# Local attention in a gated cross-attention network: where the inverse norms of the query and key heads are computed, and when their unit vectors are made

## The chip, the cores and the metric

The kernel runs on one core of one Trainium2 chip. A core has TensorE (PE in the profile), VectorE (DVE), ScalarE (ACT), GpSimd (POOL) and SyncE (SP, which here issues the DMAs). The metric is the device time of one execution, in microseconds (us). The kernel before took 3235.11 us, the median of three runs from 3233.68 to 3237.66.

## The reference, cut to what matters

Two gated cross-attentions and a feed-forward network come first. The last part, in which the change lies, is a local transformer of two layers on 2048 tokens of 256 features, with 8 heads of 64 and windows of 128 tokens. Its attention does this:

```python
qkv = shift_token(x) @ wqkv                      # 256 -> 3 * 512
q, k, v = heads(qkv)
q = q / clip(norm(q), 1e-12) * q_scale           # k likewise
q, k = rotary_xpos(q, k)                         # x*cos*scale + rotate_half(x)*sin*scale
# window w attends to its own 128 keys and those of window w-1
sim = mask(8 * q_w @ [k_{w-1}, k_w].T)
o_w = softmax(sim) @ [v_{w-1}, v_w]
x = x + concat(o) @ wo
```

After it comes a gated feed-forward network, and then the second layer.

## The kernel before, in words

The local transformer is `local_transformer`, and its attention is `windowed_attention`, called once per layer. Tokens lie on the 128 partitions, one window per tile (`Z[:, w, :]`), and a window is the unit of work: 16 of them in each layer. Each engine has a program of its own, written out in Python in the order in which it is to run. The engines meet only through semaphores (`s["..."]`); `after(engine, name, count)` is a wait, and `.then_inc` a signal. The order of the calls in each engine's loop `for w in range(ST + 1)` (ST is 16) therefore sets the order of the work. Iteration w works on several windows at once: it projects window w+3, rotates w+2, turns w+1, scores w, and adds the result of w-1.

The path of one window through the engines:

- PE turns the tokens (`turn_input`, L1983), ACT copies them out of PSUM (`move_input`, L2093 and L2097), and POOL splits them into a high and a low fp16 part (`split_input`, L67 and L71).
- PE projects queries and keys (`project_qk`, L77 to L79) into two PSUM banks; ACT squares the 1024 numbers of a token (`square`, L2104); DVE sums the squares of each of the 16 heads into `norms[:, 0, :]` (`sum_squares`, L2238).
- ACT takes the root of these 16 numbers (`root`, L2124). Square root and exponential need different activation tables, so a table load stands before the root and another before the next exponential.
- DVE clips, inverts and multiplies (`make_unit`, L2177, L2179, L2182); the unit vectors are 128x1024. With this the PSUM banks are free for the next projection.
- DVE multiplies them by the cosine table (`straighten`, L2223), POOL by the sine table (`cross`, L2310), and DVE adds the two (`rotate`, L2245). PE turns the result (`turn`, L1974) and ACT copies it as `qT` and `kT` (`move`, L2085 and L2086).
- PE scores (`score`, L1934, or L1939 where the two key tiles are not neighbours in the ring); DVE masks and takes the maxima, in two groups of four heads (`mask` L2206, `maxima` L2214); ACT takes the exponentials with their sums (`expo`, L2071).
- DVE inverts the eight sums (`invert`, L2191) and POOL spreads them over 64 columns a head (`expand`, L2331). PE turns this by four matmuls against the identity (`spread`, L2026), and ACT copies it (`move_spread`, L2079).
- PE turns the probabilities (`turn_probs`, L2002), ACT copies them (`move_probs`, L2117), and PE applies them to the values (`apply`, L2016).
- DVE multiplies the output by the spread inverses (`normalize`, L2198), PE mixes it with `wo` (`mix`, L1990), and DVE adds it to the tokens (`add`, L2231).

In iterations 2 to 10 DVE also splits one part of the feed-forward weights into high and low fp16 (`split_weights`: L59 and L63).

Of the kernel before, what the change touches and what calls it, by code (L numbers as in the profile page):

```python
# [1440 lines left out]
def narrow_attention(nc, m, rows_d, ctxT_d, wq_d, wk_d, wv_d, wo_d, bqk_d, bv_d, bo_d, q_parts, k_parts, pw):  # L1441
# [390 lines left out]


V_RING, K_RING, Z_RING = 6, 4, 3

RAW, W1_PARTS, W2_PARTS = 3, 6, 3
SPLIT_AT = range(2, 2 + W1_PARTS + W2_PARTS)
# [2 lines left out]
HEAD_AT = [4 * (p // 4) + 2 * (p % 2) + (p // 2) % 2 for p in range(LH)]  # L1840
ATTENTION_SIGNALS = (
    "scored", "qk_projected", "v_projected", "turned", "spread", "in_turned", "mixed", "probs_turned", "applied",
    "exped", "spread_moved", "moved", "in_moved", "squared", "valued", "probs_moved", "rooted",
    "clipped", "inverted", "united", "weighed", "expanded", "normed", "masked", "maxed", "straightened", "added", "summed",
    "rotated", "crossed", "in_split", "in_hi", "tables_in", "rest_in", "scaled", "cleared")


# [37 lines left out]
def windowed_attention(nc, m, name, Z, pw, wm, w, l, s):  # L1885

    base = l * ST
    with ExitStack() as own:
# [8 lines left out]
        unit = [sb(f"unit{i}", [P, 2, LH, 2, LD // 2]) for i in range(2)]  # L1897
        straight, crossed = sb("straight", [P, 2, LH, LD]), sb("crossed", [P, 2, LH, 2, LD // 2])
        rotated = [sb(f"rotated{i}", [P, 2 * INNER]) for i in range(2)]
        norms = sb("norms", [P, 4, 16])  # L1900
        scores, probs = sb("scores", [P, LH, 2 * P]), sb("probs", [P, LH, 2 * P])
        probsT = [sb(f"probsT{i}", [P, 4, 2, P]) for i in range(2)]
        minus_max, sums, inverse = sb("minus_max", [P, LH]), sb("sums", [P, LH]), sb("inverse", [P, LH])
# [7 lines left out]
        def after(engine, sem, count):  # L1911
            if count > 0:
                engine.wait_ge(s[sem], count)

        with nc.Block() as block:
# [5 lines left out]
            def _(pe):  # L1921
# [55 lines left out]

                def turn_input(w):

                    after(pe, "normed", base + w - 4)  # L1980
                    after(pe, "in_moved", base + w)
                    for k in range(DK):
                        last = nc.tensor.transpose(m.PS[:, OUT_BANK, k * P:(k + 1) * P], Z[:, w, k * P:(k + 1) * P], m.ident[:])  # L1983
                    last.then_inc(s["in_turned"], 1)
# [57 lines left out]
                for w in range(ST + 1):  # L2042
                    if inside(w):
                        score(w)
                    if inside(w + 3):
                        project_qk(w + 3)
                    if inside(w - 1):
                        if w == 1:
                            pe.wait_ge(s["rest_in"], 32 * (l + 1))
                        mix(w - 1)  # L2050
                    if inside(w + 1):
                        turn(w + 1)
                    if inside(w + 3):
                        project_v(w + 3)
                    if inside(w + 4):
                        turn_input(w + 4)
                    if inside(w):
                        for g in range(2):
                            turn_probs(w, g)
                        apply(w)  # L2060
                        spread(w)

            @block.scalar
            def _(act):
# [10 lines left out]
                def move_spread(w):  # L2075

                    after(act, "spread", base + w + 1)
                    after(act, "normed", base + w)
                    nc.scalar.activation(spread_in[:].rearrange("p c n -> p (c n)"), m.PS[:, OUT_BANK, :],  # L2079
                                         ACT.Copy).then_inc(s["spread_moved"], 1)  # L2080
# [49 lines left out]
                value(0)  # L2130
                root(0)
                move_input(2)
                square(1)
                value(1)
                root(1)
                move_input(3)
                square(2)
                move(0)
                value(2)
                root(2)  # L2140
                for w in range(ST + 1):
                    if inside(w - 1):
                        move_spread(w - 1)
                    if inside(w):
                        expo(w, 0)
                        expo(w, 1)
                    if inside(w + 1):
                        move(w + 1)
                    if inside(w + 4):
                        move_input(w + 4)  # L2150
                    if inside(w + 3):
                        square(w + 3)
# [6 lines left out]
                    if inside(w + 3):  # L2159
                        root(w + 3)  # L2160

            @block.vector
            def _(dve):
# [8 lines left out]

                def make_unit(w):

                    after(dve, "rooted", base + w + 1)
                    after(dve, "united", base + w)
                    nc.vector.tensor_scalar(norms[:, 2, :], norms[:, 1, :], 1e-12 * FF_SCALE, None, ALU.max).then_inc(s["clipped"], 1)  # L2177
                    dve.wait_ge(s["clipped"], base + w + 1)
                    nc.vector.reciprocal(norms[:, 3, :], norms[:, 2, :]).then_inc(s["inverted"], 1)  # L2179
                    dve.wait_ge(s["inverted"], base + w + 1)  # L2180
                    after(dve, "crossed", base + w - 1)
                    nc.vector.tensor_tensor(  # L2182
                        unit[w % 2][:].rearrange("p q h a d -> p (q h) (a d)"),
                        m.PS[:, qk_bank(w):qk_bank(w) + 2, :].rearrange("p b (h d) -> p (b h) d", d=LD),
                        norms[:, 3, :].unsqueeze(2).to_broadcast([P, 16, LD]), ALU.mult).then_inc(s["united"], 1)

                def invert(w):

# [45 lines left out]
                def sum_squares(w):  # L2234

                    after(dve, "squared", base + w + 1)
                    after(dve, "clipped", base + w)
# [27 lines left out]
                dve.wait_ge(s["tables_in"], 32 * (l + 1))  # L2265
                scale_tables(0, 2)
                scale_tables(2, ST)
                sum_squares(0)
                for w in (0, 1):
                    make_unit(w)  # L2270
                    straighten(w)
                    sum_squares(w + 1)
                    rotate(w)
                for w in range(ST + 1):
                    if inside(w + 2):
                        make_unit(w + 2)
                    if inside(w - 1):
                        normalize(w - 1)
                    if inside(w):
                        if w == 0:  # L2280
                            dve.wait_ge(s["rest_in"], 32 * (l + 1))
                        for g in range(2):
                            mask(w, g)
                            maxima(w, g)
                    if inside(w - 1):
                        add(w - 1)
                    if inside(w + 2):
                        straighten(w + 2)
                    if inside(w + 2):
                        rotate(w + 2)  # L2290
                    if inside(w):
                        invert(w)
                    if inside(w + 3):
                        sum_squares(w + 3)
                    if w in SPLIT_AT:
                        split_weights(SPLIT_AT.index(w))

            @block.gpsimd
            def _(pool):
                nc.gpsimd.memset(kT[:, :, K_RING - 1, :], 0.0)  # L2300
                nc.gpsimd.memset(V[:, V_RING - 1, :, :], 0.0).then_inc(s["cleared"], 1)

                def cross(w):
# [21 lines left out]
                def expand(w):  # L2325
# [11 lines left out]
                split_input(1)  # L2337
                split_input(2)
                cross(0)
                cross(1)  # L2340
                split_input(3)
                for w in range(ST + 1):
                    if inside(w + 2):
                        cross(w + 2)
                    if inside(w):
                        expand(w)
                    if inside(w + 4):
                        split_input(w + 4)


LN_PARTS = ("shifted", "shift_moved", "first_half", "counted", "step", "root_wanted", "root_done", "staged", "h_turned",
# [425 lines left out]
```

## Time and profile before

| | |
|---|---|
| median of three runs | 3235.11 us |
| the profiled execution's own time | 3229.91 us |
| its span | 3227.8 us |
| PE busy over the span | 2967.1 us (92%) |
| DVE busy | 2208.0 us (68%) |
| ACT busy | 1982.0 us (61%) |
| POOL busy | 218.4 us (7%) |

The span is the stretch from the first to the last recorded instruction of the profiled execution, and its own time lies 2.1 us above it. The busy shares are means over stages with different limits. The attention of the two local layers stands from about 2424 to 2702 us and again from about 2822 to 3099 us, minus the feed-forward part between. In a timeline each row gives the start, the duration, the engine, the line, the operation, what it writes and reads, the number of instructions merged in it, and in brackets how long the engine had idled before and what released it.

### The profile page before, as it was taken

Reading aid. Unit: us, or ns where it says so; the run is one execution under the profiler, and the core shown is the slowest. Engines: PE = TensorE matmul, PEld = TensorE weight load, DVE = VectorE, ACT = ScalarE, POOL = GpSimd, SP = SyncE. Lnnn points to the kernel's source line nnn. Section 1 sums busy time; section 2 is a strip of 40 time slices with the busy share of each in tenths; the row PEclk is TensorE's granted clock in tenths of the full one; section 3 lists DMA queues with packets and bytes.
Section 4 is the critical chain, followed back from the end, with each engine's and each line's share of the span. In section 5 each row is a group of like instructions: output and inputs, shape, how many; then the busy total and the mean of one; then the engine's idle time right before and its main releaser. Section 6 shows DMA issues by size and latency. Waiting matters only on the chain. (4 is left out here: it accounts for less than half of the span.)

```text
span 3227.8 us, 71016 instructions
## 1 busy us (share of the span) xinstructions
PE 2967.1 (92%) x29442; PEld 1483.9 (46%) x29442; DVE 2208.0 (68%) x2752; ACT 1982.0 (61%) x2682; POOL 218.4 (7%) x325
## 2 busy tenths in 40 slices
PE   6999999999999999999999887999977887988878
PEld 3444444444444444444444563222235665556655
DVE  6888788878888888878788854000027775677756
ACT  5665655655656656556556424999965773267732
POOL 0000000000000000000000102000004223042200
PEclk8999999999999999999999898999998998999989
DMA  2000000000000000000000003110010001000000
GB/s 78 7 2 2 8 2 8 2 2 8 2 2 8 2 2 8 2 3 2 2 3 2 31 3 126 27 36 27 28 44 20 17 1 58 3 16 17 1 1 27
DMA packets 30033, 51.65 MB, mean 16 GB/s; under 512 B 6071, under 2 KB 22538, under 8 KB 28554
## 3 DMA queue, kind: packets, MB, share of 16 engines
q1 hardware_dynamic: 29706, 46.91, 4.6%
q8 instruction: 252, 4.13, 0.5%
q14 instruction: 75, 0.61, 0.1%
HBM read 41.04 MB, written 5.83 MB: 15 GB/s over the span
## 5 line engine op out<-in xcount | busy, mean ns | idle before, releaser
L734 ACT ACTIVATE a_probs<-PS 128x1024 f32<-128x1024 f32 x928 | 949.1, 1024 | 601.2 <-PE PS L489 597.4
L502 PE MATMUL PS<-a_probs,a_V 64*64 64x512 f32 x7424 | 977.8, 590 | 5.0 <-DVE a_heads_outT L915 3.6
L956 DVE TENSOR_TENSOR a_prob_sums<-a_prob_sums,a_probs 128x1024 f32<-128x1024 f32 x512 | 627.1, 1225 | 153.8 <-ACT a_probs L734 137.8
L953 DVE SCALAR_TENSOR_TENSOR a_prob_sums<-a_probs,a_valid,a_prob_sums 128x1024 f32<-128x1024 f32 x384 | 480.4, 1251 | 70.2 <-ACT a_probs L734 60.3
L489 PE MATMUL PS<-a_Q_hi,a_K_hi 64*64 64x512 f16 x3712 | 383.9, 381 | 5.0 <-ACT a_probs L734 4.7
L1772 ACT ACTIVATE c_probs<-PS 128x1024 f32<-128x1024 f32 (+1 forms) x416 | 382.8, 1080 | 8.3 <-PE PS L1691 6.7
L489 PE MATMUL PS<-a_Q_lo,a_K_hi 64*64 64x512 f16 x3712 | 383.5, 377 | 2.5 <-issue 2.5
L489 PE MATMUL PS<-a_Q_hi,a_K_lo 64*64 64x512 f16 x3712 | 381.1, 377 | 1.3 <-issue 1.3
L502 PEld LDWEIGHTS PS<-a_probs,a_V 64*64 64x64 f32 x7424 | 288.5, 133 | 164.1 <-issue 20.4
L489 PEld LDWEIGHTS PS<-a_Q_hi,a_K_hi 64*64 64x64 f16 x3712 | 118.4, 106 | 275.8 <-issue 270.7
L489 PEld LDWEIGHTS PS<-a_Q_hi,a_K_lo 64*64 64x64 f16 x3712 | 119.0, 107 | 228.3 <-issue 226.4
L1711 PE MATMUL PS<-c_probs,c_Vh 128*32 128x512 f32 (+1 forms) x1664 | 222.5, 607 | 0.3 <-ACT c_probs L1772 0.3
L1790 DVE COPY c_outT<-PS 128x512 f32<-128x512 f32 x16 | 11.1, 691 | 303.3 <-PE PS L1711 303.3
L1691 PE MATMUL PS<-c_Qop,c_Kop 64*128 64x512 f16 (+1 forms) x832 | 155.6, 390 | 34.6 <-ACT c_probs L1772 11.3
L2071 ACT ACTIVATE d_probs<-d_scores,d_minus_max 128x256 f32<-128x256 f32 x256 | 127.0, 497 | 88.2 <-DVE d_minus_max L2214 88.2
L489 PEld LDWEIGHTS PS<-a_Q_lo,a_K_hi 64*64 64x64 f16 x3712 | 120.0, 107 | 92.7 <-issue 7.8
L1691 PEld LDWEIGHTS PS<-c_Qop,c_Kop 64*128 64x128 f16 (+1 forms) x832 | 38.7, 94 | 250.9 <-ACT c_probs L1772 236.8
L923 DVE RECIPROCAL a_inverse<-PS 128x128 f32<-128x128 f32 x128 | 121.5, 950 | 27.1 <-PE PS L512 27.1
L71 POOL TENSOR_TENSOR b_W_lo<-b_W1T,b_W_hi 128x256 f16<-128x256 f32 x8 | 8.1, 1044 | 1830.9 <-DVE b_W_hi L67 1830.9
L2002 PE MATMUL PS<-ident,d_probs 128*128 128x128 f32 x512 | 70.3, 296 | 48.2 <-ACT d_kT L2086 41.5
L2310 POOL TENSOR_TENSOR d_crossed<-d_unit,d_tables 128x256 f32<-128x256 f32 x128 | 92.7, 758 | 147.8 <-DVE d_unit L2182 147.8
L2002 PEld LDWEIGHTS PS<-ident,d_probs 128*128 128x128 f32 x512 | 62.2, 153 | 56.2 <-issue 48.3
(325 smaller groups left out, 4227.5 us busy)
## 6 DMA issues: line engine op xcount, KB each, us to landing
c_Qop<-q_part SPq DMA_DIRECT2D x96, 64.0 KB, 2.3
c_Kop<-k_part SPq DMA_DIRECT2D x96, 50.0 KB, 2.0
d_raw<-in_l1f_w_dram SPq DMA_DIRECT2D x18, 256.0 KB, 3.2
d_tables<-in_rotary_dram SPq DMA_DIRECT2D x2, 2048.0 KB, 11.0
X<-in_x_dram SPq DMA_DIRECT2D x2, 1024.0 KB, 9.5
out_dram<-X SPq DMA_DIRECT2D x4, 512.0 KB, 3.5
c_cT<-in_ctxT_dram SPq DMA_DIRECT2D x1, 1601.0 KB, 6.4
a_probs<-in_ctx_dram SPq DMA_DIRECT2D x3, 512.0 KB, 5.0
```

What stands on the lines that cost most here:

```text
L489: last = nc.tensor.matmul(m.PS[64 * g:64 * g + 64, 2 * (n % 2) + h, :], k[rows, half_keys], q[rows, queries], start=(j == 0), stop=(j == l ...
L502: last = nc.tensor.matmul(m.PS[64 * h:64 * h + 64, PVB + g, :], V[e][rows, s, 64 * h:64 * h + 64], probs[n % 4][rows, h * BANK:(h + 1) * B ...
L734: nc.scalar.activation(probs[n % 4][:], m.PS[:, b0:b0 + 2, :].rearrange("p b c -> p (b c)"), ACT.Exp).then_inc(exped, 1)
L923: nc.vector.reciprocal(inverse[:, part], m.PS[:, TOTAL, part]).then_inc(inverted, 1)
L953: nc.vector.scalar_tensor_tensor(out=sums, in0=new, scalar=valid[:, s:s + 1], in1=sums, op0=ALU.mult, op1=ALU.add).then_inc(summed, 1)
L956: nc.vector.tensor_tensor(sums, sums, new, ALU.add).then_inc(summed, 1)
L1691: last = nc.tensor.matmul(m.PS[0:r, STEP_BANKS[n] + b, :], Kop[e][rows, c0:c0 + r], Qop[e][rows, q0:q0 + BANK], start=True, stop=True)
L1711: last = nc.tensor.matmul(m.PS[32 * q:32 * q + 32, 4 + e, :], Vh[e][0:r, t % CT, :], probs[2 * (t % 2) + q // 2][0:r, (q % 2) * BANK:(q % ...
L1772: nc.scalar.activation(probs[2 * (t % 2) + hp][0:r, :], m.PS[0:r, STEP_BANKS[n]:STEP_BANKS[n] + 2, :].rearrange("p b c -> p (b c)"), ACT.E ...
L2002: last = nc.tensor.transpose(m.PS[:, SCORE_BANK + 2 * g + p // 2, at:at + P], probs[:, 4 * g + p, kt * P:(kt + 1) * P], m.ident[:])
L2071: last = nc.scalar.activation(probs[:, p, :], scores[:, p, :], ACT.Exp, bias=minus_max[:, p:p + 1], accum_out=sums[:, p:p + 1])
L2310: last = nc.gpsimd.tensor_tensor(crossed[:, qk, :, a, :], unit[w % 2][:, qk, :, 1 - a, :], tables[:, 1, w, qk, a * 32:a * 32 + 32].unsquee ...
```

## The change

The square root leaves ACT. POOL now clips the sums of squares and raises them to the power -0.5 (`power`, two instructions on 128x16), and DVE refines that by one Newton step, y(1.5 - 0.5 x y^2), in three instructions on 128x16 in place of the clip and the reciprocal. `make_unit(w + 3)` stands at the end of iteration w, where `make_unit(w + 2)` stood at the start of the iteration. DVE's `invert(w)` goes ahead of `rotate(w + 2)`. On ACT `square(w + 3)` goes ahead of `move_input(w + 4)`, `move_spread(w)` comes at the end of iteration w in place of the start of the next, and the table for the exponential is loaded before the loop. On PE `spread(w)` goes ahead of `apply(w)` and consists of transposes in place of matmuls. `turn_input` waits for `spread_moved` in place of `normed`.

```diff
-        norms = sb("norms", [P, 4, 16])
+        norms, minus_half = sb("norms", [P, 6, 16]), sb("minus_half", [P, 16])
...
-                    after(pe, "normed", base + w - 4)
+                    after(pe, "spread_moved", base + w - 4)
...
-                        last = nc.tensor.matmul(m.PS[:, OUT_BANK, c * P:(c + 1) * P],
-                                                expanded[:, c].rearrange("p e d -> p (e d)"), m.ident[:], start=True, stop=True)
+                        last = nc.tensor.transpose(m.PS[:, OUT_BANK, c * P:(c + 1) * P],
+                                                   expanded[:, c].rearrange("p e d -> p (e d)"), m.ident[:])
...
+                        spread(w)
                         apply(w)
-                        spread(w)
...
-                def root(w):
-
-                    after(act, "summed", base + w + 1)
-                    nc.scalar.activation(norms[:, 1, :], norms[:, 0, :], ACT.Sqrt).then_inc(s["rooted"], 1)
-
-                act.wait_ge(s["cleared"], 2 * (l + 1))
+                nc.scalar.preload_act_table(ACT.Exp)
+                act.wait_ge(s["cleared"], 3 * (l + 1))
...
-                    after(dve, "rooted", base + w + 1)
-                    after(dve, "united", base + w)
-                    nc.vector.tensor_scalar(norms[:, 2, :], norms[:, 1, :], 1e-12 * FF_SCALE, None, ALU.max).then_inc(s["clipped"], 1)
-                    dve.wait_ge(s["clipped"], base + w + 1)
-                    nc.vector.reciprocal(norms[:, 3, :], norms[:, 2, :]).then_inc(s["inverted"], 1)
-                    dve.wait_ge(s["inverted"], base + w + 1)
+                    squared, first, product, step, root = (norms[:, i, :] for i in range(5))
+                    steps = NORM_STEPS * (base + w)
+                    dve.wait_ge(s["powered"], base + w + 1)
+                    nc.vector.scalar_tensor_tensor(out=product, in0=squared, scalar=SQUARE_CLIP, in1=first, op0=ALU.max,
+                                                   op1=ALU.mult).then_inc(s["norm_step"], 1)
+                    dve.wait_ge(s["norm_step"], steps + 1)
+                    nc.vector.scalar_tensor_tensor(out=step, in0=first, scalar=-0.5, in1=product, op0=ALU.mult,
+                                                   op1=ALU.mult).then_inc(s["norm_step"], 1)
+                    dve.wait_ge(s["norm_step"], steps + 2)
+                    nc.vector.scalar_tensor_tensor(out=root, in0=step, scalar=1.5, in1=first, op0=ALU.add,
+                                                   op1=ALU.mult).then_inc(s["norm_step"], 1)
+                    dve.wait_ge(s["norm_step"], steps + 3)
...
-                sum_squares(0)
                 for w in (0, 1):
+                    sum_squares(w)
                     make_unit(w)
                     straighten(w)
-                    sum_squares(w + 1)
                     rotate(w)
+                sum_squares(2)
+                make_unit(2)
...
                     if w in SPLIT_AT:
                         split_weights(SPLIT_AT.index(w))
+                    if inside(w + 3):
+                        make_unit(w + 3)
...
+                def power(w):
+
+                    if w == 0:
+                        pool.wait_ge(s["cleared"], 3 * (l + 1))
+                    after(pool, "summed", base + w + 1)
+                    after(pool, "united", base + w)
+                    nc.gpsimd.tensor_scalar(norms[:, 5, :], norms[:, 0, :], SQUARE_CLIP, None, ALU.max).then_inc(s["limited"], 1)
+                    pool.wait_ge(s["limited"], base + w + 1)
+                    nc.gpsimd.tensor_tensor(norms[:, 1, :], norms[:, 5, :], minus_half[:], ALU.pow).then_inc(s["powered"], 1)
+
...
                     if inside(w + 4):
                         split_input(w + 4)
+                    if inside(w + 3):
+                        power(w + 3)
```

ACT, one iteration from the first copy after the exponentials to the next exponentials. Before:

```order
L2085 ACTIVATE d_qT<-PS 128x512
L2086 ACTIVATE d_kT<-PS 128x4x128
L2093 ACTIVATE d_zw<-PS 128x2x128
L2097 ACTIVATE d_zw<-PS 128x1
L2104 ACTIVATE d_squares<-PS 128x1024
L2117 ACTIVATE d_probsT<-PS 128x1024
L2111 ACTIVATE d_V<-PS 128x512
L2117 ACTIVATE d_probsT<-PS 128x1024
L2124 ACT_TABLE_LOAD
L2124 ACTIVATE d_norms<-d_norms 128x16
L2079 ACTIVATE d_spread_in<-PS 128x512
L2071 ACT_TABLE_LOAD
```

The same stretch of ACT after the change (the lines of the functions are one or so higher):

```order
L2086 ACTIVATE d_qT<-PS 128x512
L2087 ACTIVATE d_kT<-PS 128x4x128
L2105 ACTIVATE d_squares<-PS 128x1024
L2094 ACTIVATE d_zw<-PS 128x2x128
L2098 ACTIVATE d_zw<-PS 128x1
L2118 ACTIVATE d_probsT<-PS 128x1024
L2112 ACTIVATE d_V<-PS 128x512
L2118 ACTIVATE d_probsT<-PS 128x1024
L2080 ACTIVATE d_spread_in<-PS 128x512
```

Both table loads and the root are gone from the loop, and the squares stand ahead of the copy of the next tokens.

DVE, from the sums of squares of iteration 2 to the first mask of iteration 3. Before:

```order
L2238 TENSOR_REDUCE d_norms<-d_squares 128x16
L59 TENSOR_SCALAR d_w_hi<-d_raw 128x4x128
L63 SCALAR_TENSOR_TENSOR d_w_lo<-d_raw,d_w_hi 128x4x128
L2177 TENSOR_SCALAR d_norms<-d_norms 128x16
L2179 RECIPROCAL d_norms<-d_norms 128x16
L2182 TENSOR_TENSOR d_unit<-PS,d_norms 128x1024
L2198 TENSOR_TENSOR d_heads_outT<-PS,d_spread_in 128x512
L2206 TENSOR_TENSOR d_scores<-PS,d_masks 128x1024
```

The same stretch of DVE after the change:

```order
L2236 TENSOR_REDUCE d_norms<-d_squares 128x16
L59 TENSOR_SCALAR d_w_hi<-d_raw 128x4x128
L63 SCALAR_TENSOR_TENSOR d_w_lo<-d_raw,d_w_hi 128x4x128
L2170 SCALAR_TENSOR_TENSOR d_norms<-d_norms 128x16
L2173 SCALAR_TENSOR_TENSOR d_norms<-d_norms 128x16
L2176 SCALAR_TENSOR_TENSOR d_norms<-d_norms 128x16
L2180 TENSOR_TENSOR d_unit<-PS,d_norms 128x1024
L2196 TENSOR_TENSOR d_heads_outT<-PS,d_spread_in 128x512
L2204 TENSOR_TENSOR d_scores<-PS,d_masks 128x1024
```

In steady state DVE's sequence is the same but for three small instructions in place of two: the unit vectors stand between the same neighbours, and only what they wait for is another engine's.

POOL, one iteration. Before:

```order
L2310 TENSOR_TENSOR d_crossed<-d_unit,d_tables 128x8x32 x4
L2331 COPY d_expanded<-d_inverse 128x256 x2
L67 CAST d_zw_hi<-d_zw 128x256
L71 TENSOR_TENSOR d_zw_lo<-d_zw,d_zw_hi 128x256
L2310 TENSOR_TENSOR d_crossed<-d_unit,d_tables 128x8x32 x4
```

The same iteration of POOL after the change:

```order
L2310 TENSOR_TENSOR d_crossed<-d_unit,d_tables 128x8x32 x4
L2331 COPY d_expanded<-d_inverse 128x256 x2
L67 CAST d_zw_hi<-d_zw 128x256
L71 TENSOR_TENSOR d_zw_lo<-d_zw,d_zw_hi 128x256
L2342 TENSOR_SCALAR d_norms<-d_norms 128x16
L2344 TENSOR_TENSOR d_norms<-d_norms,d_minus_half 128x16
L2310 TENSOR_TENSOR d_crossed<-d_unit,d_tables 128x8x32 x4
```

The two instructions of `power` stand behind the split of the next tokens.

## Rows read from the trace of the kernel before

**Rows 1.** Stretches: us, busy time and instructions of each engine, granted clock, DMA.
```profile
2466.80:2651.60 184.80, 165.60 (x1346) 124.26 (x1342) 142.66 (x188) 145.61 (x334) 53.44 (x95) 1.00 0.03 10
```
**Rows 2.** Timeline of DVE, one iteration of the first layer's attention.
```profile
2511.28 1.22 DVE L2182 TENSOR_TENSOR d_unit<-PS,d_norms 128x1024 f32<-128x1024 f32 x1
...
2513.02 1.21 DVE L2206 TENSOR_TENSOR d_scores<-PS,d_masks 128x1024 f32<-128x1024 f32 x1
...
2520.81 0.19 DVE L2191 RECIPROCAL d_inverse<-d_sums 128x8 f32<-128x8 f32 x1
2522.22 1.22 DVE L2238 TENSOR_REDUCE d_norms<-d_squares 128x16 f32<-128x1024 f32 x1 [1.22 <-ACT d_squares L2104]
2523.36 0.42 DVE L59 TENSOR_SCALAR d_w_hi<-d_raw 128x512 f16<-128x512 f32 x1
2523.81 0.69 DVE L63 SCALAR_TENSOR_TENSOR d_w_lo<-d_raw,d_w_hi 128x512 f16<-128x512 f32 x1
2526.18 0.17 DVE L2177 TENSOR_SCALAR d_norms<-d_norms 128x16 f32<-128x16 f32 x1 [1.68 <-ACT d_norms L2124]
...
2526.68 1.22 DVE L2182 TENSOR_TENSOR d_unit<-PS,d_norms 128x1024 f32<-128x1024 f32 x1
```
**Rows 3.** Timeline of ACT, the same iteration.
```profile
2519.89 0.57 ACT L2085 ACTIVATE d_qT<-PS 128x512 f32<-128x512 f32 x1
...
2521.16 1.03 ACT L2104 ACTIVATE d_squares<-PS 128x1024 f32<-128x1024 f32 x1
...
2523.59 1.03 ACT L2117 ACTIVATE d_probsT<-PS 128x1024 f32<-128x1024 f32 x1
2524.64 1.28 ACT L2124 ACT_TABLE_LOAD   x1
2525.94 0.21 ACT L2124 ACTIVATE d_norms<-d_norms 128x16 f32<-128x16 f32 x1
```
**Rows 4.** Timeline of PE, the same iteration.
```profile
2521.09 1.94 PE L2002 MATMUL PS<-ident,d_probs 128*128 128x128 f32 x16 [0.73 <-ACT d_kT L2086]
2523.76 2.01 PE L2016 MATMUL PS<-d_probsT,d_V 128*64 128x128 f32 x32 [0.73 <-ACT d_V L2111]
2525.70 1.16 PE L2026 MATMUL PS<-ident,d_expanded 128*128 128x128 f32 x8
```
**Rows 5.** Timeline of POOL, first at the layer's start, then in the same iteration.
```profile
2448.42 1.52 POOL L71 TENSOR_TENSOR d_zw_lo<-d_zw,d_zw_hi 128x256 f16<-128x256 f32 x1
...
2521.76 0.40 POOL L67 CAST d_zw_hi<-d_zw 128x256 f16<-128x256 f32 x1
2522.24 0.67 POOL L71 TENSOR_TENSOR d_zw_lo<-d_zw,d_zw_hi 128x256 f16<-128x256 f32 x1
```
**Rows 6.** Timeline of DVE beside the first of the POOL rows above.
```profile
2449.35 0.63 DVE L2177 TENSOR_SCALAR d_norms<-d_norms 128x16 f32<-128x16 f32 x1
```
**Rows 7.** Groups of instructions on POOL by shape: count, busy us, mean ns, idle before.
```profile
L1384 POOL TENSOR_SCALAR f_qkv_raw<-f_qkv_raw 128x512 f32<-128x512 f32 x6 | 9.6, 1630 | 5.4 <-DMA f_qkv_raw<-in_l1f_wqkv_dram 5.4
...
L2652 POOL COPY d_shift<-ident 128x1 f32<-128x1 f32 x1 | 0.2, 250 | 0.0
```
**Rows 8.** Timeline of DVE and POOL at the start of layer one, then layer two.
```profile
2434.20 1.22 DVE L2238 TENSOR_REDUCE d_norms<-d_squares 128x16 f32<-128x1024 f32 x1 [3.95 <-ACT d_squares L2104]
...
2437.50 3.73 POOL L2310 TENSOR_TENSOR d_crossed<-d_unit,d_tables 128x256 f32<-128x256 f32 x4 [0.29 <-DVE d_unit L2182]
...
2451.44 1.21 DVE L2206 TENSOR_TENSOR d_scores<-PS,d_masks 128x1024 f32<-128x1024 f32 x1
...
2833.34 0.18 DVE L2177 TENSOR_SCALAR d_norms<-d_norms 128x16 f32<-128x16 f32 x1 [1.18 <-ACT d_norms L2124]
```
**Rows 9.** Timeline of PE and DVE in the last iterations of layer one.
```profile
2663.23 2.64 PE L2016 MATMUL PS<-d_probsT,d_V 128*64 128x128 f32 x32
2665.80 1.16 PE L2026 MATMUL PS<-ident,d_expanded 128*128 128x128 f32 x8
...
2668.24 1.21 DVE L2206 TENSOR_TENSOR d_scores<-PS,d_masks 128x1024 f32<-128x1024 f32 x1
```

More of the change, by code:

```diff
@@ L1834 @@
 V_RING, K_RING, Z_RING = 6, 4, 3
+NORM_STEPS, SQUARE_CLIP = 3, (1e-12 * FF_SCALE) ** 2
 RAW, W1_PARTS, W2_PARTS = 3, 6, 3
@@ L1842 @@
     "scored", "qk_projected", "v_projected", "turned", "spread", "in_turned", "mixed", "probs_turned", "applied",
-    "exped", "spread_moved", "moved", "in_moved", "squared", "valued", "probs_moved", "rooted",
-    "clipped", "inverted", "united", "weighed", "expanded", "normed", "masked", "maxed", "straightened", "added", "summed",
+    "exped", "spread_moved", "moved", "in_moved", "squared", "valued", "probs_moved",
+    "norm_step", "limited", "powered", "united", "weighed", "expanded", "normed", "masked", "maxed", "straightened", "added", "summed",
     "rotated", "crossed", "in_split", "in_hi", "tables_in", "rest_in", "scaled", "cleared")
@@ L2130, in _ @@
                 value(0)
-                root(0)
                 move_input(2)
@@ L2134, in _ @@
                 value(1)
-                root(1)
                 move_input(3)
@@ L2139, in _ @@
                 value(2)
-                root(2)
                 for w in range(ST + 1):
-                    if inside(w - 1):
-                        move_spread(w - 1)
                     if inside(w):
@@ L2148, in _ @@
                         move(w + 1)
+                    if inside(w + 3):
+                        square(w + 3)
                     if inside(w + 4):
                         move_input(w + 4)
-                    if inside(w + 3):
-                        square(w + 3)
                     if inside(w):
@@ L2158, in _ @@
                         move_probs(w, 1)
-                    if inside(w + 3):
-                        root(w + 3)
+                        move_spread(w)
             @block.vector
@@ L2184, in make_unit @@
                         m.PS[:, qk_bank(w):qk_bank(w) + 2, :].rearrange("p b (h d) -> p (b h) d", d=LD),
-                        norms[:, 3, :].unsqueeze(2).to_broadcast([P, 16, LD]), ALU.mult).then_inc(s["united"], 1)
+                        root.unsqueeze(2).to_broadcast([P, 16, LD]), ALU.mult).then_inc(s["united"], 1)
                 def invert(w):
@@ L2236, in sum_squares @@
                     after(dve, "squared", base + w + 1)
-                    after(dve, "clipped", base + w)
+                    after(dve, "united", base + w)
                     nc.vector.tensor_reduce(norms[:, 0, :], squares[:], AX.X, ALU.add).then_inc(s["summed"], 1)
@@ L2267, in _ @@
                 scale_tables(2, ST)
-                sum_squares(0)
                 for w in (0, 1):
+                    sum_squares(w)
                     make_unit(w)
                     straighten(w)
-                    sum_squares(w + 1)
                     rotate(w)
+                sum_squares(2)
+                make_unit(2)
                 for w in range(ST + 1):
-                    if inside(w + 2):
-                        make_unit(w + 2)
                     if inside(w - 1):
@@ L2288, in _ @@
                         straighten(w + 2)
+                    if inside(w):
+                        invert(w)
                     if inside(w + 2):
                         rotate(w + 2)
-                    if inside(w):
-                        invert(w)
                     if inside(w + 3):
@@ L2300, in _ @@
                 nc.gpsimd.memset(kT[:, :, K_RING - 1, :], 0.0)
+                nc.gpsimd.memset(minus_half[:], -0.5).then_inc(s["cleared"], 1)
                 nc.gpsimd.memset(V[:, V_RING - 1, :, :], 0.0).then_inc(s["cleared"], 1)
@@ L2334, in expand @@
                     last.then_inc(s["expanded"], 1)
+                def power(w):
[6 more added lines that the diff above has]
+                    nc.gpsimd.tensor_tensor(norms[:, 1, :], norms[:, 5, :], minus_half[:], ALU.pow).then_inc(s["powered"], 1)
                 split_input(0)
                 split_input(1)
+                power(0)
                 split_input(2)
                 cross(0)
+                power(1)
                 cross(1)
                 split_input(3)
+                power(2)
                 for w in range(ST + 1):
@@ L2348, in _ @@
                         split_input(w + 4)
+                    if inside(w + 3):
+                        power(w + 3)
 LN_PARTS = ("shifted", "shift_moved", "first_half", "counted", "step", "root_wanted", "root_done", "staged", "h_turned",
```

## The prediction

> **What bounds the kernel now.** I read the table of stretches first, to see where the changed code runs and what each engine does there, then the timelines of one iteration on DVE, ACT, PE and POOL side by side. In the twelve iterations between 2466.8 and 2651.6 us PE is busy 165.6 of 184.8 us, 13.8 in each iteration, DVE 11.9, ACT 12.1 and POOL 4.5 [rows 1]. No engine is full, yet the iterations keep one period: from the unit vectors at 2511.28 to those at 2526.68 it is 15.40 us [rows 2]. So a chain from engine to engine sets it. Let T be the moment at which ACT starts the copy of `qT`, 2519.89 [rows 3]. In times after T:
>
> - 1.27 squares; 4.75 table load, 1.28 long; 6.05 root [rows 3]; 6.29 DVE clips, after 1.68 idle, and 6.79 makes unit vectors [rows 2].
> - Unit vectors and the normalisation behind them take 1.74 together (2511.28 to 2513.02), so the first mask starts at 8.53. From a first mask to the next T it is 6.87 (2513.02 to 2519.89) [rows 2, 3]. 8.53 + 6.87 = 15.40: the chain closes.
>
> The reader is to see that DVE waits for a root of 16 numbers because that root stands behind ACT's copies and a table load. A second path runs beside it: PE starts `apply` at T+3.87, after the copy of V, and `spread` at 5.81 [rows 4]; the score comes behind that.
>
> **The change, part by part.** ACT: one root and two table loads go in each iteration. The load before the root is on the chain, the one before the exponentials lies in ACT's idle time and is worth nothing. The squares go ahead of the two copies of tokens and start at T+0.96 in place of 1.27, since those took the 0.31 between; they end at 1.99, and DVE sums them from 2.02 to 3.16 (1.14 each, 2522.22 to 2523.36 [rows 2]). `invert` now starts at about T+0.15 in place of 0.92; its signal leads through POOL's copies (which may have to stand behind the rotation) to `spread` by about 2.2, ahead of its turn on PE, so it costs nothing.
>
> POOL: the token copies now end on ACT at about 2.43. The cast then runs from 2.48, and the low part from 2.96 to 3.63 (0.48 and 0.67 as in [rows 5]). Behind it stand the two new instructions. For the first, a maximum, I take 0.25, what the one-column copy took [rows 7]. The price of the power, p, the trace does not show. From below it is 0.25, the same row. From above I take 1.63, the dearest POOL instruction of the local layers, on 32 times as many columns [rows 7]. I take p = 0.75. It lies below the middle because a two-input POOL instruction on 256 columns costs 0.67 [rows 5], so 16 columns bring little of their own and what is left is the arithmetic of a power; this is the weakest number of the sum. No gain from below is possible, since the instruction is new.
>
> In an iteration without `split_weights` the maximum runs from 3.70 to 3.95 and the power from 4.02 to 4.02 + p. DVE then does three small instructions, which I put at 0.21 each (clip and reciprocal took 0.50 together, 2526.18 to 2526.68 [rows 2]), so unit vectors start at 4.73 + p, and the mask at 6.47 + p. PE's path gives a floor: `spread` is moved into the gap of 0.73 before `apply` [rows 4] and its four transposes cost about 4 x 0.12 = 0.48 (sixteen took 1.94) in place of 1.09 (2525.70 less the next score), so `apply` still starts at 3.87, lasts 1.94, and the first half of the score, 1.0, is ready for DVE near 7.0. With p = 0.75 the mask comes at 7.22, the period is 7.22 + 6.87 = 14.09, a gain of 1.31; in general 2.06 - p, at most 1.53. PE needs 13.8 - 0.6 = 13.2 and stays below it.
>
> In the nine iterations with `split_weights` DVE and POOL meet. What the trace shows of that: the same low-part subtraction took 1.52 in place of 0.67 when it met DVE's rotation [rows 5], and the DVE clip behind it took 0.63 in place of 0.17 [rows 6, 2], ending with the POOL instruction. They do not share, they take turns. Here `w_hi` (0.42) becomes ready at 3.16 while POOL subtracts until 3.63, and runs to 4.05; POOL's maximum, ready at 3.70, gets its turn at 4.05 and ends at 4.28; `w_lo` (0.69) was ready by then and runs to 4.97; the power, ready at 4.33, starts at 4.97. Unit vectors start at 5.68 + p, the mask at 7.42 + p, and the gain is 15.40 - 14.29 - p = 1.11 - p, or 0.36. The Trainium skill, page "SBUF — State Buffer", section "SBUF: two separate sides", says that DVE (with two SBUF inputs or in a two-port mode) and GpSimd take one shared port pair as an exclusive lock, the first holding it for its whole instruction. By that rule the times are those above, and the trace agrees (0.63 and 1.52); without it the nine iterations would gain 1.31 like the others. The rule speaks against putting a tiny POOL instruction on the path while DVE splits weights.
>
> Start of a layer: before, the sum of `w = 1` and its root stood under POOL's `cross`. Now each window runs through in sequence. Before, first sum to first mask is 17.24 (2434.20 to 2451.44 [rows 8]). After: twice (sum 1.20, power and Newton 1.08 + p, unit 1.25, cross 3.80, rotation 1.15), then sum, power and Newton, and unit, 3.48 + p. That is 20.44 + 3p, a loss of 3.2 + 3p. In the second layer a table load made DVE wait 1.18 in place of 0.28 [rows 8], so the loss is 0.9 less.
>
> End of a layer: in the last three iterations there are no roots. `spread` and its copy stood behind `apply`. `apply` ended at 2665.80, the mask came at 2668.24 [rows 9]; now `apply`, whose second half waits for the second copy of probabilities, ends about the same, the score follows at once and is half done 1.0 later: about 2667.0, a gain of 1.2. Twice that, and 1.7 for the last normalisation, which waits only for `apply`: 4.1 a layer.
>
> Sum with p = 0.75: a layer has 13 intervals from first mask to first mask in which norms are still made, nine with a weight split and four without. Nine x 0.36 = 3.2, four x 1.31 = 5.2, end 4.1, start -5.45: 7.1 in the first layer, 8.0 in the second, together 15.1. In general 39.1 - 32p, which is zero at p = 1.22. The profiled execution's own 3229.9 would become 3214.8. It lies 5.2 below the median of the runs, 3235.1, so for the median I say 3220.0.
>
> **The rivals.**
> - No turns in the split iterations. If POOL's small instructions slip in between DVE's, the nine gain 1.31 too: 2 x 9 x 0.95 = 17.1 more, 3202.9. For it: `w_lo` has to be issued after `w_hi` signals, and there the order could fall the other way. Against it: both collisions above. With p = 0.25 and no turns all 13 gain 1.53, and each layer's start costs 1.5 less: 19.9 + 4.1 - 3.95 and 0.9 better in layer two, 41 in all, 3194.
> - Slower: the power is dear. It stands on the path of each of the 32 windows, so each microsecond of it costs 32. Above p = 1.42 the kernel is slower by over 6.5 us; at 1.63 it takes 3248. At 3 us, which no row excludes, the path still goes through POOL: 39.1 - 96 = -57, 3292. For it: POOL takes 2.6 ns a column for one subtraction, and a power is many operations. Against it: 16 columns are few.
> - The gain is given back: p between 1.02 and 1.42, where the steady iterations win a little and the two starts lose as much: 3235.
> - That the table loads stay is excluded by the instruction order, which has none in the loop.
>
> **How the numbers follow.** Forecast, turns taken and p below 1.02: 0.38. No turns with p up to about 1.3: 0.20. Given back: 0.16. Dear power up to 1.63: 0.18; dearer: 0.08. Within 0.2% (6.5 us) is about what a measurement of this kernel can tell from no change. Faster is 0.58, same 0.16, slower 0.26. The range goes from the cheap power without turns, 3194, to the power at its upper bound with the turns, 3250; the forecast's own range is 3206 (p = 0.25, turns) to 3229.
>
> **What would show it right or wrong.** In the changed profile: L2344 at 0.25 to 1.0 us; the period between rows of L2180 at 14.1 in iterations without L59 and 15.0 with it; in the latter L2344 starting only when L63 ends, and L59 stretched by the POOL subtraction; no ACT_TABLE_LOAD between exponentials; from the first L2236 to the first L2204 22.7 in place of 17.24; L2027 under 0.6 in place of 1.1. The forecast is wrong if L2344 takes over 1 us, if DVE waits before L2170 for something else than POOL, or if both kinds of iteration have one period.

## The result, and the profile after

The changed kernel takes 3280.02 us (median of 4 runs, 3277.17 to 3284.07), the kernel before in the same session 3236.39. The ratio is 1.0137, 95% interval 1.0125 to 1.015: it is slower, by 43.6 us. I had said 3220.0, and 3250 at most.

The cause stands in one row. This is the timeline of POOL in the changed kernel, one iteration without a weight split (the first three rows) and one with it:

```profile
2490.58 0.67 POOL L71 TENSOR_TENSOR d_zw_lo<-d_zw,d_zw_hi 128x256 f16<-128x256 f32 x1
2491.33 0.25 POOL L2342 TENSOR_SCALAR d_norms<-d_norms 128x16 f32<-128x16 f32 x1
2491.67 2.93 POOL L2344 TENSOR_TENSOR d_norms<-d_norms,d_minus_half 128x16 f32<-128x16 f32 x1
...
2506.71 0.67 POOL L71 TENSOR_TENSOR d_zw_lo<-d_zw,d_zw_hi 128x256 f16<-128x256 f32 x1
2507.47 0.31 POOL L2342 TENSOR_SCALAR d_norms<-d_norms 128x16 f32<-128x16 f32 x1
2507.86 3.32 POOL L2344 TENSOR_TENSOR d_norms<-d_norms,d_minus_half 128x16 f32<-128x16 f32 x1
```

The power (L2344) takes 2.93 us on 16 columns, over four times the 0.67 of a subtraction on 256 columns, and 3.32 beside DVE's weight split. DVE waits for it. The timeline of DVE in the changed kernel, the iteration that belongs to the last rows, answers to [rows 2]:

```profile
2505.87 1.22 DVE L2236 TENSOR_REDUCE d_norms<-d_squares 128x16 f32<-128x1024 f32 x1 [0.54 <-ACT d_squares L2105]
2507.01 0.66 DVE L59 TENSOR_SCALAR d_w_hi<-d_raw 128x512 f16<-128x512 f32 x1
2507.70 0.69 DVE L63 SCALAR_TENSOR_TENSOR d_w_lo<-d_raw,d_w_hi 128x512 f16<-128x512 f32 x1
2511.22 0.17 DVE L2170 SCALAR_TENSOR_TENSOR d_norms<-d_norms 128x16 f32<-128x16 f32 x1 [2.82 <-POOL d_norms L2344]
2511.42 0.17 DVE L2173 SCALAR_TENSOR_TENSOR d_norms<-d_norms 128x16 f32<-128x16 f32 x1
2511.63 0.17 DVE L2176 SCALAR_TENSOR_TENSOR d_norms<-d_norms 128x16 f32<-128x16 f32 x1
2511.84 1.22 DVE L2180 TENSOR_TENSOR d_unit<-PS,d_norms 128x1024 f32<-128x1024 f32 x1
...
2528.42 1.22 DVE L2180 TENSOR_TENSOR d_unit<-PS,d_norms 128x1024 f32<-128x1024 f32 x1
```

The period is 16.58 (2511.84 to 2528.42) in place of 15.40. Where DVE had idled 1.68 for ACT, it idles 2.82 for POOL. What was planned besides came. T, the moment at which ACT starts the copy of `qT`, is 2503.86 here, from the timeline of ACT in the changed kernel:

```profile
2503.86 0.57 ACT L2086 ACTIVATE d_qT<-PS 128x512 f32<-128x512 f32 x1
```

So the sum of squares starts at T+2.01 (0.32 earlier), and the Newton step costs 0.62 (2511.22 to 2511.84). The timeline of PE in the changed kernel, the same iteration, answers to [rows 4]:

```profile
2505.07 1.94 PE L2003 MATMUL PS<-ident,d_probs 128*128 128x128 f32 x16 [1.07 <-ACT d_kT L2087]
2506.84 0.60 PE L2027 MATMUL PS<-ident,d_expanded 128*128 128x128 f32 x4
2507.73 2.01 PE L2017 MATMUL PS<-d_probsT,d_V 128*64 128x128 f32 x32 [0.29 <-ACT d_V L2112]
2509.68 2.00 PE L1935 MATMUL PS<-d_kT,d_qT 64*128 64x256 f32 x16
```

The spread is four records of 0.60 together in place of eight of 1.16. It fills the gap ahead of `apply`, and the score starts at T+5.82 in place of 6.9. PE is early, and nothing asks for it: DVE masks at T+9.72 (2513.58).

The start of a layer, the timeline of DVE in the changed kernel (answers to [rows 8]):

```profile
2434.65 1.22 DVE L2236 TENSOR_REDUCE d_norms<-d_squares 128x16 f32<-128x1024 f32 x1 [3.16 <-ACT d_squares L2105]
2439.34 0.35 DVE L2170 SCALAR_TENSOR_TENSOR d_norms<-d_norms 128x16 f32<-128x16 f32 x1 [3.47 <-POOL d_norms L2344]
...
2451.37 0.17 DVE L2170 SCALAR_TENSOR_TENSOR d_norms<-d_norms 128x16 f32<-128x16 f32 x1 [3.39 <-POOL d_norms L2344]
...
2462.95 0.17 DVE L2170 SCALAR_TENSOR_TENSOR d_norms<-d_norms 128x16 f32<-128x16 f32 x1 [3.39 <-POOL d_norms L2344]
...
2464.72 1.21 DVE L2204 TENSOR_TENSOR d_scores<-PS,d_masks 128x1024 f32<-128x1024 f32 x1
```

Three windows wait in a row: from the first sum to the first mask it is 30.07 in place of 17.24.

By stretch, from rows of both traces (start, from the first sum to the first mask; 13 intervals, from the first window's first mask to the 14th's; end, from there to the last normalisation):

| | start | 13 intervals | end | sum |
|---|---|---|---|---|
| layer one, before | 17.24 | 200.15 | 46.78 | |
| layer one, after | 30.07 | 213.46 | 42.77 | |
| difference | +12.8 | +13.3 | -4.0 | +22.1 |
| layer two, difference | +11.9 | +13.4 | -3.6 | +21.7 |

Together +43.8. The medians lie 43.6 apart. The two profiled executions lie 47.5 apart (spans of 3275.3 and 3227.8), and 3.2 of the rest stand in the feed-forward part between the layers, 135.8 us at a granted clock of 0.92 in place of 132.6 at 0.95; that the change causes them is not shown. DVE's waits for L2344 sum to 100.0 us over the 32 windows.

### The profile page after: what moved, and what is told of

It is laid out like the page before. It is cut to its first block and busy times, and to the rows that moved or that the text cites. A ratio compares the mean times of both kernels' runs of the same rounds, so it can differ in the third digit from the quotient of the medians.

```text
span 3275.3 us, 70774 instructions
## 1 busy us (share of the span) xinstructions
PE 2962.6 (90%) x29314; PEld 1471.9 (45%) x29314; DVE 2215.4 (68%) x2784; ACT 1904.3 (58%) x2597; POOL 355.2 (11%) x391
## 5 line engine op out<-in xcount | busy, mean ns | idle before, releaser
L1790 DVE COPY c_outT<-PS 128x512 f32<-128x512 f32 x16 | 11.1, 692 | 303.5 <-PE PS L1711 303.5
L77 PE MATMUL PS<-qkv_hi,d_zw_lo 128*128 128x512 f16 x192 | 77.3, 403 | 65.4 <-DVE d_unit L2180 54.3
L2344 POOL TENSOR_TENSOR d_norms<-d_norms,d_minus_half 128x16 f32<-128x16 f32 x32 | 100.8, 3151 | 2.7
```

Source lines behind the costliest of these rows:

```text
L77: nc.tensor.matmul(out, sl, mh, start=start, stop=False)
L2344: nc.gpsimd.tensor_tensor(norms[:, 1, :], norms[:, 5, :], minus_half[:], ALU.pow).then_inc(s["powered"], 1)
```

## The experiments

Theory P: what was wrong is the price of the power; the other terms of the sum hold. Rival O: the new orders cost time by themselves. Each diff is cut to the lines that matter. The kernel before took 3233.19 us beside the first four and 3232.71 beside the last four.

**A cheap operation in the power's place.** The norms are other numbers then; nothing else is changed.

```diff
-                nc.gpsimd.memset(minus_half[:], -0.5).then_inc(s["cleared"], 1)
+                nc.gpsimd.memset(minus_half[:], 1e-4).then_inc(s["cleared"], 1)
...
-                    nc.gpsimd.tensor_tensor(norms[:, 1, :], norms[:, 5, :], minus_half[:], ALU.pow).then_inc(s["powered"], 1)
+                    nc.gpsimd.tensor_tensor(norms[:, 1, :], norms[:, 5, :], minus_half[:], ALU.mult).then_inc(s["powered"], 1)
```

> The changed kernel with a multiplication by 0.0001 in place of the power, of the same shape and with the same waits (the norms come out as other numbers; nothing else is changed). Theory P, the price of the power is what was wrong in the prediction and the rest of its sum holds: L2344 takes 0.25 to 0.3 us instead of 2.93 to 3.32; the iterations without a weight split have a period of 13.9, those with one about 14.2 to 14.6, each layer's start (first sum to first mask) about 21.3, and the kernel takes 3200 to 3210 us. Rival O, the new order costs time by itself (the norms in sequence at the start, the swapped order on PE and ACT): the period stays above 15 or the starts above 25, and the time is 3225 us or more.

Measured: 3196.78 us, ratio 0.989 (0.9873 to 0.9906). With the multiplication the change saves 36.4 us, with the power it costs 43.6, each against the kernel before in its own session: the one instruction is worth 80 us and turns the change from faster to slower. The time is 3 us below the range expected. The timeline of DVE, two masks without a weight split between them, and then two with one:

```profile
2458.91 1.21 DVE L2204 TENSOR_TENSOR d_scores<-PS,d_masks 128x1024 f32<-128x1024 f32 x1
...
2472.76 1.22 DVE L2204 TENSOR_TENSOR d_scores<-PS,d_masks 128x1024 f32<-128x1024 f32 x1 [0.30 <-PE PS L1935]
...
2514.50 1.23 DVE L2204 TENSOR_TENSOR d_scores<-PS,d_masks 128x1024 f32<-128x1024 f32 x1
...
2528.39 1.22 DVE L2204 TENSOR_TENSOR d_scores<-PS,d_masks 128x1024 f32<-128x1024 f32 x1
```

The first interval is 13.85, and DVE ends it waiting 0.30 for PE's score: the floor that I had put at 13.87. With a split it is 13.89, not 14.2 to 14.6. The start of layer one is 21.92 (2436.99 to 2458.91), 0.6 longer than expected. The rows of POOL and then of DVE say why the split costs so little:

```profile
2510.24 0.67 POOL L71 TENSOR_TENSOR d_zw_lo<-d_zw,d_zw_hi 128x256 f16<-128x256 f32 x1
2510.99 0.30 POOL L2342 TENSOR_SCALAR d_norms<-d_norms 128x16 f32<-128x16 f32 x1
2511.38 0.62 POOL L2344 TENSOR_TENSOR d_norms<-d_norms,d_minus_half 128x16 f32<-128x16 f32 x1
...
2510.52 0.67 DVE L59 TENSOR_SCALAR d_w_hi<-d_raw 128x512 f16<-128x512 f32 x1
2511.23 0.69 DVE L63 SCALAR_TENSOR_TENSOR d_w_lo<-d_raw,d_w_hi 128x512 f16<-128x512 f32 x1
```

The cheap instruction takes 0.62 beside the weight split and 0.22 at its shortest: it is held for 0.40 and ends 0.08 after DVE's subtraction (2512.00 and 2511.92). The maximum is held for 0.05 only (0.30, not 0.25), because it comes up just 0.20 before the high half ends (2510.99 and 2511.19), and it ends 0.10 after it. So the engines do hold one another up, for some 0.45 in all and not for the 0.95 that I had worked out.

**DVE makes the inverse root.** POOL's two instructions go; DVE clips, guesses from the bits and takes two Newton steps.

```diff
+                    chain(nc.vector.tensor_scalar(limit, squared, SQUARE_CLIP, None, ALU.max))
+                    chain(nc.vector.tensor_scalar(guess.bitcast(int32), limit.bitcast(int32), -0.5, float(0x5f3759df),
+                                                  ALU.mult, ALU.add))
+                    for source, target in ((guess, better), (better, guess)):
+                        chain(nc.vector.tensor_tensor(product, limit, source, ALU.mult))
+                        chain(nc.vector.scalar_tensor_tensor(out=step, in0=source, scalar=-0.5, in1=product,
+                                                             op0=ALU.mult, op1=ALU.mult))
+                        chain(nc.vector.scalar_tensor_tensor(out=target, in0=step, scalar=1.5, in1=source,
+                                                             op0=ALU.add, op1=ALU.mult))
```

> The changed kernel with POOL's two instructions gone: DVE makes the inverse root itself, by a clip, a guess from the bits of the number (one multiply-add on its integer view) and two Newton steps, eight instructions on 128x16 in a row. Theory P: 8 x 0.205 = 1.65 us replace the wait for POOL; iterations without a weight split 13.9, with one 14.8; starts about 22.3; the kernel takes 3210 to 3218 us, faster than before. Rival O as for the other run: 3225 us or more. If DVE's small instructions cost more in a dependent row than 0.205, the period shows it directly.

Measured: 3214.66 us, ratio 0.9943 (0.9927 to 0.996), inside the range expected. From its timeline of DVE, the first two and the last of the eight and the unit vectors:

```profile
2515.25 0.17 DVE L2177 TENSOR_SCALAR d_norms<-d_norms 128x16 f32<-128x16 f32 x1
2515.45 0.17 DVE L2178 TENSOR_SCALAR d_norms<-d_norms 128x16 int32<-128x16 int32 x1
...
2516.70 0.17 DVE L2184 SCALAR_TENSOR_TENSOR d_norms<-d_norms 128x16 f32<-128x16 f32 x1
2516.91 1.22 DVE L2188 TENSOR_TENSOR d_unit<-PS,d_norms 128x1024 f32<-128x1024 f32 x1
```

Eight instructions take 1.66 (2515.25 to 2516.91), 0.21 each. The period is 14.72 with a split, 13.87 without, and the start 23.11, 0.8 longer than expected.

**The root on ACT, in the new order.**

```diff
-                        move_spread(w)
+                    if inside(w + 3):
+                        root(w + 3)
+                    if inside(w):
+                        move_spread(w)
...
-                    dve.wait_ge(s["powered"], base + w + 1)
+                    after(dve, "rooted", base + w + 1)
```

> The changed kernel with only the power undone: ACT takes the root again, behind the second copy of the probabilities and ahead of the spread copy, with its table loads, and DVE clips and inverts; all the new orders and the transposed spread stay. Theory P: the chain over ACT is as in the kernel before, so 15.4 in both kinds of iteration; start 3 longer than before in each layer, end 4 shorter; 3230 to 3237 us, no change from before. Rival O: slower than before by over 10 us. Rival Q, the new order is worth a gain of its own in steady state: under 3225 us.

Measured: 3230.3 us, ratio 0.9995 (0.9985 to 1.0004): no change. Its unit vectors come at 2503.41 and 2518.82, 15.41 apart; DVE idles 1.77 for ACT. The period is the old one, so rivals O and Q fall for the steady iterations. At the ends of a layer the new orders do act, and cancel: the starts are 19.77 and 20.93, which is 2.5 and 2.8 longer than before, and the ends 43.21 and 43.07, which is 3.6 and 2.2 shorter.

**The power alone, in the old order** (the new `power` and Newton step put into the kernel before).

> The kernel before with only the root replaced, by the power on POOL and the Newton step on DVE; the orders of PE, ACT and DVE and the spread by matmuls stay as before. Theory P: L2344's counterpart takes 2.9 to 3.3 us; the period is 16.2 without a weight split and 16.6 with one; no gain at the end; the start, where the second sum runs ahead of the rotation, 9 to 10 longer than before; 3278 to 3290 us. Rival O, under which the new orders cost: 3268 us or less.

Measured: 3280.49 us, ratio 1.0149 (1.0132 to 1.0166). It is as slow as the whole change: period 16.66 with a split (normalisations at 2498.12 and 2514.78), 16.18 without. The starts are 27.80 and 27.76, which is 10.6 and 9.6 longer than before, the first a little more than expected. The loss does not need the new orders.

**The spread alone.**

```diff
-                        last = nc.tensor.matmul(m.PS[:, OUT_BANK, c * P:(c + 1) * P],
-                                                expanded[:, c].rearrange("p e d -> p (e d)"), m.ident[:], start=True, stop=True)
+                        last = nc.tensor.transpose(m.PS[:, OUT_BANK, c * P:(c + 1) * P],
+                                                   expanded[:, c].rearrange("p e d -> p (e d)"), m.ident[:])
...
+                        spread(w)
                         apply(w)
-                        spread(w)
```

> The kernel before with one edit on PE: the spread goes ahead of the application of the probabilities and consists of transposes. Theory P: in steady iterations the chain over ACT's root is untouched, period 15.4; in the last three iterations of a layer, where no root is made, the normalisation waits only for the application: 4 us less in each layer, 8 together, 3225 us. Rival N, nothing: PE's share is hidden at the end as well, 3233. Rival S: the spread of the inverses now waits for POOL ahead of the application and delays it, slower than before.

Measured: 3224.82 us, ratio 0.9975 (0.9965 to 0.9985): 7.9 us faster. The period is 15.40 still; from the 13th normalisation to the 16th of layer one it is 43.30, where before it was 47.38. The timeline of DVE in this run, then in the kernel before:

```profile
2655.90 0.68 DVE L2198 TENSOR_TENSOR d_heads_outT<-PS,d_spread_in 128x512 f32<-128x512 f32 x1
...
2699.20 0.69 DVE L2198 TENSOR_TENSOR d_heads_outT<-PS,d_spread_in 128x512 f32<-128x512 f32 x1 [3.52 <-PE PS L2016]
...
2650.99 0.68 DVE L2198 TENSOR_TENSOR d_heads_outT<-PS,d_spread_in 128x512 f32<-128x512 f32 x1
...
2698.37 0.69 DVE L2198 TENSOR_TENSOR d_heads_outT<-PS,d_spread_in 128x512 f32<-128x512 f32 x1 [6.09 <-ACT d_spread_in L2079]
```

The last normalisation waits for PE's `apply` and no longer for the copy of the spread, as expected. The term of the end is shown by itself, 4.1 in layer one and 3.4 in layer two (41.90 in place of 45.25), and rivals N and S fall. This part of the change paid. How much of it the place of the spread brings and how much the transposes, no run separates.

**The power on 32 columns.**

```diff
-                    nc.gpsimd.tensor_tensor(norms[:, 1, :], norms[:, 5, :], minus_half[:], ALU.pow).then_inc(s["powered"], 1)
+                    nc.gpsimd.tensor_tensor(norms[:, 1:3, :], norms[:, 5:6, :].to_broadcast([P, 2, 16]),
+                                            minus_half[:].unsqueeze(1).to_broadcast([P, 2, 16]), ALU.pow).then_inc(s["powered"], 1)
```

> The changed kernel with the power on 32 columns in place of 16 (the first 16 are used, the other 16 repeat them). If the price is by the column, 0.17 to 0.18 us each, L2344 takes 5.6 to 5.8 us where DVE leaves it alone, the period grows by 2.8 and the kernel takes 3360 to 3372 us. If it is a fixed price of the instruction (a routine that is fetched or started), it stays near 3.0 and the kernel at 3280.

Measured, one run: 3366.26 us. The timeline of POOL at the start of layer one:

```profile
2450.42 0.25 POOL L2342 TENSOR_SCALAR d_norms<-d_norms 128x16 f32<-128x16 f32 x1 [2.55 <-DVE d_norms L2236]
2450.76 5.46 POOL L2344 TENSOR_TENSOR d_norms<-d_norms,d_minus_half 128x32 f32<-128x32 f32 x1
```

The price is by the column: (5.46 - 2.93) / 16 = 0.158 us each, and about 0.4 for the instruction (2.93 - 16 x 0.158), a line drawn through two sizes only, of which the wider reads its columns twice. The period without a split grows by just what the instruction grew, 2.53 (18.67 against 16.14), less than the 2.8 expected. That the time is in the range all the same is in part luck. Nine of the 26 intervals were 0.9 to 1.3 us longer than the others of their kind, at a granted clock of 0.83 to 0.85. In one of them (2566.86 to 2587.14) PE's projections stood 0.43 us apart in place of 0.21, and DVE waited 2.11 for `mix`. The nine add some 10 us to the time.

**DVE's inverse root with the old start.**

```diff
-                for w in (0, 1):
-                    sum_squares(w)
+                sum_squares(0)
+                for w in (0, 1):
                     make_unit(w)
                     straighten(w)
+                    sum_squares(w + 1)
                     rotate(w)
-                sum_squares(2)
                 make_unit(2)
```

> The kernel with DVE's eight small instructions in place of the power, and with the start of a layer as in the kernel before (the second and third sum ahead of the rotation). Theory P: steady iterations stay at 13.9 and 14.7; the start loses 3 us less in each layer, 20 in place of 23.1; 3208 to 3211 us.

Measured: 3209.43 us, ratio 0.9924 (0.9906 to 0.9941), as expected. The start is 21.08 (2434.62 to 2455.70) in place of 23.11: 2.0 less and not 3.

**And the high half of the weights on ACT**, as the last run but with

```diff
+                    nc.scalar.activation(hi, raw, ACT.Copy, scale=FF_SCALE).then_inc(s["w_hi"], 1)
...
-                    scaled_hi(nc.vector, hi, raw).then_inc(s["w_hi"], 1)
```

> As the run before it, and the high half of each weight part is made by ACT behind its copy of the spread inverses, one iteration ahead, so that DVE only subtracts. Theory P: DVE's path in the nine iterations with a weight split loses 0.45 for the high half and 0.24 of its wait for POOL: period 14.0 in place of 14.7, 12 us in all, 3196 to 3200 us. Rival: the high half delays ACT's exponentials or the subtraction meets POOL's, and the period stays near 14.5: 3205 us or more.

Measured: 3200.39 us, ratio 0.9898 (0.9881 to 0.9916), the fastest of the versions that compute the true norms, 1% below the kernel before. The timeline of DVE:

```profile
2511.49 1.22 DVE L2226 TENSOR_TENSOR d_scores<-PS,d_masks 128x1024 f32<-128x1024 f32 x1
...
2521.49 0.93 DVE L63 SCALAR_TENSOR_TENSOR d_w_lo<-d_raw,d_w_hi 128x512 f16<-128x512 f32 x1
...
2525.74 1.22 DVE L2226 TENSOR_TENSOR d_scores<-PS,d_masks 128x1024 f32<-128x1024 f32 x1
```

The period is 14.25, not 14.0: the wait of 0.24 for POOL's subtraction did not go, it passed from the high half to the low one (0.93 in place of 0.69; POOL's subtraction ends at 2521.87).

## Why the prediction was wrong

- **The chain and the load that leaves it: right.** With the root on ACT the period is 15.4 in either order; with a cheap instruction in its place it is 13.9.
- **The price of the power: the step that failed.** I bounded p by 0.25 and 1.63 and took 0.75, on the ground that "16 columns bring little of their own". It is 2.93. The upper bound was the dearest POOL row at hand, which says nothing of another operation: that row moves 512 columns at 3.2 ns each, and a power takes 158 ns a column. By my own formula each microsecond of p costs 32, so the miss of 2.2 turns a gain of 15.1 into a loss of 54.7; measured is a loss of 43.6. The run with the multiplication and the one with the power alone show that nothing else made the loss. The rival of the dear power had the mechanism and, for 3 us, the time: 3292 forecast, 3280 measured. It had 0.08, and I kept it outside the range. The bounds were no bounds, and the range leaned on them.
- **Turns in the split iterations: right in kind, too large in size.** I charged 0.95; the whole difference between the two kinds of iteration is 0.44 (16.58 against 16.14, 2480.26 to 2496.40). `w_hi`, the maximum and the power, which I had waiting, all did wait. But each ended later than the one it waited for by its own time less 0.13 or 0.14: `w_hi` 0.29 after POOL's subtraction (2507.67 and 2507.38; alone it takes 0.42), the maximum 0.11 after `w_hi` (2507.78; alone 0.25), the power 2.79 after `w_lo` (2511.18 and 2508.39; alone 2.93). This comes out within 0.02 us in each of the 18 split iterations. The lock rule of the Trainium skill (page "SBUF — State Buffer", section "SBUF: two separate sides"), by which the first of two such instructions holds the shared ports to its end, agrees with these rows but for the 0.13 to 0.14. My sum laid the full times end to end, though [rows 5, 6] had the clip end only 0.04 after POOL's subtraction (2449.98 and 2449.94; alone 0.17). It also had `w_lo` wait for the maximum and end at T+4.97; `w_lo` started at T+3.84, took its own 0.69 and ended at T+4.53. Of the turns 0.06 is left for the maximum and 0.39 for the power.
- **What this makes of the sum:** with p = 2.93 it gives a loss of 54.7, and the table above shows 43.8. The 26 intervals were charged 13.0 too much (9.2 of it the turns, 18 x 0.51), the starts 1.7 too little, and the gain at the ends was 0.6 less.
- **Iterations without a split:** 13.34 + p gives 16.27; 16.14 measured. The floor by PE, 13.87, was 13.85.
- **The start:** 3.2 + 3p and 2.3 + 3p give 12.0 and 11.1; 12.8 and 11.9 measured. Most of the 0.8 is the first Newton step: 1.15 from 2439.34 to 2440.49 in place of 0.62, beside POOL's split of the next tokens. With the old order of the sums and DVE's eight instructions it is 2 us less in each layer.
- **The end:** 4.1 forecast, 4.0 and 3.6 measured; by itself 4.1 and 3.4, and 7.9 in the time.
- **The spread's transposes:** under 0.6 in place of 1.1 forecast, 0.60 in place of 1.16 measured.

## What to carry to other kernels

An operation that no row of the trace shows has no upper bound from rows of other operations: when it stands on the path of every window, its price decides the sign, and the range must reach to where that price would put it. Moving a small computation off a busy engine helps only if the new place is quick to answer; here eight dependent instructions of 0.21 us on DVE beat one of 2.93 on an idle POOL. Where a change bundles several edits, price each by the stretch that it acts in: the spread's place and form acted only in the last three of 16 windows. And where two engines take turns, full times must not be laid end to end: here each turn came out 0.13 to 0.14 us shorter than the instruction by itself, a large part of one that takes 0.2 to 0.4.

## What the runs showed of the hardware that I had not expected

- POOL's power of two tensors takes 0.158 us a column on 128 partitions and some 0.4 fixed (2.93 on 16 columns, 5.46 on 32, no other size measured), whereas the same instruction with a multiplication took 0.22 on 16.
- DVE takes the inverse root in 1.66 us on 16 columns by a multiply-add on the integer view of the number and two Newton steps.
- Where a DVE and a POOL instruction took turns, the later one ended 0.13 to 0.14 us sooner after the first than its own time. It is the same for 0.22 us (the multiplication, 2512.00 after 2511.92), 0.25, 0.42 and 2.93, so it does not grow with the instruction; no run shows its cause.
- The two POOL copies of 128x256 that used to take 0.74 together took 1.66 behind DVE's rotation (2504.26 on POOL, L2331), which cost nothing, since PE asks for them later.
